# Expert weights in transfers of two experts, with eight experts' weights in memory

## What is computed

```python
logits = x @ gate_weight.T                      # 2048 tokens, 64 experts
scores = softmax(logits)
# the 3 best of 8 groups of experts are kept, and of these the 6 best experts of a token
flat = topk_i.reshape(-1)
pos = place of the token in its expert's queue
slot = flat * C + minimum(pos, C - 1)           # C = 96 places for each expert
buf = zeros((E * C, H)).at[slot].set(x[tok]).reshape(E, C, H)
g = einsum('ech,emh->ecm', buf, Wg)             # M = 176
u = einsum('ech,emh->ecm', buf, Wu)
out = einsum('ecm,ehm->ech', silu(g) * u, Wd)
y = sum over a token's 6 slots of out[slot] * topk_w
shared = (silu(x @ Sg.T) * (x @ Su.T)) @ Sd.T
return y + shared
```

## Time and profile before

| | us |
|---|---|
| median of 3 runs | 1223.92 |
| lowest and highest run | 1222.77, 1226.18 |
| the profiled execution, its time | 1213.88 |
| its span, from first to last instruction | 1212.1 |
| PE busy in the span | 1052.0 (87%) |
| mean granted clock of TensorE | 0.962 |

### The profile page before, as it was taken

One profiled execution on the slowest core, in us unless ns is written; L12 is line 12 of the kernel. 1 busy time (PEld: TensorE's weight loads), 2 busy tenths in 40 slices (PEclk: granted clock), 3 DMA queues, 4 the chain that ended last, 5 costly groups with the idle time before them and its releaser, 6 DMA issues.

```text
span 1212.1 us, 17812 instructions
## 1 busy us (share of the span) xinstructions
PE 1052.0 (87%) x5809; PEld 868.6 (72%) x5809; DVE 629.9 (52%) x1225; ACT 487.4 (40%) x864; POOL 401.6 (33%) x593
## 2 busy tenths in 40 slices
PE   4749999999999899999999999999787978777774
PEld 4538998898888789989788889888554545444443
DVE  3525455648586566678655767855564211111116
ACT  1315555555454445554544555544220122222220
POOL 2112222223225722222662322284106144344440
PEclk9969999999999999999999999999988998999995
DMA  9950000000001200000110000002010288999966
GB/s 367 328 179 0 0 0 0 1 1 27 11 1 45 90 1 1 35 1 1 66 48 1 1 36 1 1 18 89 9 44 3 63 218 212 225 226 227 232 141 211
DMA packets 58757, 95.74 MB, mean 79 GB/s; under 512 B 7771, under 2 KB 41318, under 8 KB 58176
## 3 DMA queue, kind: packets, MB, share of 16 engines
q1 hardware_dynamic: 46880, 80.66, 21.0%
q0 software_dynamic: 11808, 14.16, 6.2%
HBM read 62.17 MB, written 40.67 MB: 85 GB/s over the span
## 4 chain that ended last, share of the span: by engine, by line
PE 62%; DMA 12%; DVE 7%; issue 6%; POOL 6%; SPq 5%; ACT 2%; POOLq 0%; DVEq 0%; ACTq 0%
PE ps L1081 18%; PE ps L1104 9%; DMA wds<-in_wd 9%; PE ps L1128 9%; PE ps L1117 7%; PE ps L1286 4%; POOL slot_rows L436 3%; PE ps L1301 3%; PE ps L1223 2%; SPq L288 2%; PE ps L1233 2%; PE ps L1090 2%; PE ps L1111 2%; PE ps L1093 2%; DMA acc<-zrow 2%
## 5 line engine op out<-in xcount | busy, mean ns | idle before, releaser
L382 POOL TENSOR_TENSOR holdp<-neghalf 128x1 f32<-128x1 f32 x139 | 30.4, 219 | 554.6 <-DVE ss L728 270.7
L526 ACT ACTIVATE prob<-ps,rn 128x512 f32<-128x512 f32 (+3 forms) x256 | 121.1, 525 | 183.2 <-PE ps L1104 183.0
L1081 PE MATMUL ps<-wh,hth 128*128 128x384 f32 x512 | 178.0, 348 | 9.8 <-DVE wl L693 4.6
L728 DVE TENSOR_REDUCE ss<-arena 128x8 f32<-128x1024 f32 x64 | 78.1, 1220 | 199.9 <-ACT arena L510 199.6
L1128 PE MATMUL ps<-vx,prob 128*128 128x129 f32 (+1 forms) x1280 | 155.8, 277 | 22.1 <-POOL prob L430 21.9
L1128 PEld LDWEIGHTS ps<-vx,prob 128*128 128x128 f32 x1280 | 154.6, 193 | 25.9 <-POOL prob L430 23.2
L1081 PE MATMUL ps<-wl,hth 128*128 128x384 f32 x512 | 172.0, 336 | 0.0
L1081 PE MATMUL ps<-wh,htl 128*128 128x384 f32 x512 | 172.0, 336 | 0.0
L1104 PE MATMUL ps<-qt,kt 128*128 128x512 f32 (+3 forms) x512 | 152.8, 442 | 19.8 <-DVE arena L747 13.0
L510 ACT ACTIVATE arena<-ps 128x1024 f32<-128x1024 f32 x64 | 65.5, 1023 | 246.5 <-PE ps L1081 246.5
L489 POOL DMA_INDIRECT acc<-wos,arena x64 | 90.1, 1408 | 146.0 <-ACT wos L628 97.7
(11 more groups left out here) (161 smaller groups left out, 1608.3 us busy)
## 6 DMA issues: line engine op xcount, KB each, us to landing
wgus<-in_wgu SPq DMA_DIRECT2D x64, 352.0 KB
wds<-in_wd SPq DMA_DIRECT2D x64, 176.0 KB
slot_rows<-pay SPq DMA_DIRECT2D x1, 7728.0 KB, 35.4
arena<-slot_rows SPq DMA_DIRECT2D x64, 120.8 KB, 3.1
warena<-in_wqkv SPq DMA_DIRECT2D x1, 4992.0 KB, 20.1
acc<-zrow SPq DMA_DIRECT2D x2, 2048.0 KB, 29.5
warena<-acc SPq DMA_DIRECT2D x8, 512.0 KB, 7.4
wos<-in_wo SPq DMA_DIRECT2D x1, 2048.0 KB, 28.3
```

The costliest lines, as they stand in the source:

```text
L526: act_(prob[:, OFF[j]:OFF[j] + w], sflat[:, OFF[j]:OFF[j] + w], ACT.Tanh, scale=rn[:, bass.ds(head(n), 1), TT + j:TT + j + 1].squeeze(1)). ...
L728: nc.vector.tensor_reduce(ss[:].rearrange("p (c i) -> p i c", c=2), sq, X, ALU.add).then_inc(s["ss_rdy"], 1)
L1081: last = mm(ps[:, i, 0:3 * DH], hp[:, k, i * P:(i + 1) * P], wp[:, k, :], start=(k == 0 and m == 0), stop=(k == KC - 1 and m == 2))
```

## The change

The weights are packed in pairs: `wgu` holds two experts in one row of 1408 words for each of 128 partitions, and `wd` two experts in one row of 1024 words, padded from 88 rows to 96 (MP), the last 8 of zeros that no matmul reads. One transfer brings the weights of one kind for two experts, 704 KB and 384 KB. Four pairs are held (WR = 8 experts): two in the old arrays `wgus` and `wds`, which keep their sizes but for the rows of `wds`; the other two in memory of attention that is dead by then: the gate and up pairs in `prob` and in `arena2` behind the rows, the down pairs in `wos` (heads 4 to 7) and in `vx`. The first two pairs are loaded at the start as before; the other two where attention ends, behind two waits more in SP's queue (`o_rdy`: PE's last product with `prob`; `x2_rdy`: the last use of `yacc`). In the loop a pair is loaded at odd u alone, when its second expert is done, and it is for the next turn of eight.

```diff
+WR = 8
+MP = 96
...
-        wgus = sb("wgus", [P, RING, KC, 2 * M])
-        wds = sb("wds", [MC, RING, 2, D])
+        wgus = sb("wgus", [P, 2, 2 * KC * 2 * M])
+        wds = sb("wds", [MP, 2, 4 * D])
...
+        wg_pair = [wgus[:, 0], wgus[:, 1], prob[:, 0:4 * KC * M], arena2[:, XR * RW:XR * RW + 4 * KC * M]]
+        wd_pair = [wds[:, 0], wds[:, 1], wos[0:MP, 4:8, :].rearrange("p a d -> p (a d)"), vx[0:MP, 1024:1024 + 4 * D]]
+        wg_of = [wg_pair[u // 2].rearrange("p (a k m) -> p a k m", a=2, k=KC)[:, u % 2] for u in range(WR)]
+        wd_of = [wd_pair[u // 2].rearrange("p (a m d) -> p a m d", a=2, m=2)[:, u % 2] for u in range(WR)]
...
-        w_in = [sem(f"w_in{i}") for i in range(RING)]
+        w_in = [sem(f"w_in{i}") for i in range(WR // 2)]
...
-            for u in range(RING):
-                sp.dma_start(wgus[:, u], wgu[u]).then_inc(w_in[u], 16)
-                sp.dma_start(wds[:, u], wd[u]).then_inc(w_in[u], 16)
+            for u in range(2):
+                sp.dma_start(wg_pair[u], wgu[u]).then_inc(w_in[u], 16)
+                sp.dma_start(wd_pair[u], wd[u]).then_inc(w_in[u], 16)
...
+            sp.dma_start(wd_pair[2], wd[2]).then_inc(w_in[2], 16)
+            sp.wait_ge(s["o_rdy"], B * H)
+            sp.dma_start(wg_pair[2], wgu[2]).then_inc(w_in[2], 16)
+            sp.dma_start(wd_pair[3], wd[3]).then_inc(w_in[3], 16)
+            sp.wait_ge(s["x2_rdy"], 2 * B)
+            sp.dma_start(wg_pair[3], wgu[3]).then_inc(w_in[3], 16)
             sp.wait_ge(s["hmod"], 2 * B)
...
-            def gate_up(base, u):
-                sp.wait_ge(s["gu_ps"], base + (u + 1))
-                sp.dma_start(wgus[:, u % RING], wgu[bass.ds(base + (RING + u), 1)].squeeze(0)).then_inc(w_in[u % RING], 16)
+            def gate_up(r, u):
+                sp.wait_ge(s["gu_ps"], r * XR + (u + 1))
+                sp.dma_start(wg_pair[u // 2], wgu[bass.ds(r * 4 + (WR // 2 + u // 2), 1)].squeeze(0)).then_inc(w_in[u // 2], 16)
...
-            def down(base, u):
-                sp.wait_ge(s["dn_ps"], base + (u + 1))
-                sp.dma_start(wds[:, u % RING], wd[bass.ds(base + (RING + u), 1)].squeeze(0)).then_inc(w_in[u % RING], 16)
+            def down(r, u):
+                sp.wait_ge(s["dn_ps"], r * XR + (u + 1))
+                sp.dma_start(wd_pair[u // 2 % 4], wd[bass.ds(r * 4 + (WR // 2 + u // 2), 1)].squeeze(0)).then_inc(w_in[u // 2 % 4], 16)
...
-                if not (last and u >= XR - RING):
-                    gate_up(base, u)
+                if not last and u % 2 == 1:
+                    gate_up(r, u)
                 if not (first and u < 2):
-                    if not (last and u - 2 >= XR - RING):
-                        down(base, u - 2)
+                    if u % 2 == 1 and not (last and u >= 2):
+                        down(r, u - 2)
                     last_row(base, u - 2)
...
-                pe.wait_ge(w_in[e % RING], 32 * use)
+                pe.wait_ge(w_in[e % WR // 2], 32 * use)
                 for k in range(KC):
-                    last = mm(ps[0:C, 1 + e % 2, 0:2 * M], xgt[:, e % 2, k, :], wgus[:, e % RING, k, :], start=(k == 0), stop=(k == KC - 1))
+                    last = mm(ps[0:C, 1 + e % 2, 0:2 * M], xgt[:, e % 2, k, :], wg_of[e % WR][:, k, :], start=(k == 0), stop=(k == KC - 1))
...
-                    last = mm(ps[0:C, 4 + e % 2, 0:D], actt[:, e % 2, m, :], wds[:, e % RING, m, :], start=(m == 0), stop=(m == 1))
+                    last = mm(ps[0:C, 4 + e % 2, 0:D], actt[:, e % 2, m, :], wd_of[e % WR][0:MC, m, :], start=(m == 0), stop=(m == 1))
...
-                gu(e, base, (XR // RING) * r + (e // RING + 1))
+                gu(e, base, r + 1)
```

More of the change, by code:

```diff
@@ L336, in last_row, with sp_period @@
                 sp.dma_start(o95_d[bass.ds(base + u, 1)], orow[C - 1:C, u % RING, :]).then_inc(o95s[u % RING], 16)
-            def down(base, u):
-                sp.wait_ge(s["dn_ps"], base + (u + 1))
-                sp.dma_start(wds[:, u % RING], wd[bass.ds(base + (RING + u), 1)].squeeze(0)).then_inc(w_in[u % RING], 16)
-            def sp_period(base, u):
-                first = isinstance(base, int) and base == 0
-                last = isinstance(base, int) and base == E - XR
-                if not (last and u >= XR - RING):
-                    gate_up(base, u)
+            def down(r, u):
+                sp.wait_ge(s["dn_ps"], r * XR + (u + 1))
+                sp.dma_start(wd_pair[u // 2 % 4], wd[bass.ds(r * 4 + (WR // 2 + u // 2), 1)].squeeze(0)).then_inc(w_in[u // 2 % 4], 16)
+            def sp_period(r, u):
+                base = r * XR
+                first = isinstance(r, int) and r == 0
+                last = isinstance(r, int) and r == E // XR - 1
+                if not last and u % 2 == 1:
+                    gate_up(r, u)
                 if not (first and u < 2):
-                    if not (last and u - 2 >= XR - RING):
-                        down(base, u - 2)
+                    if u % 2 == 1 and not (last and u >= 2):
+                        down(r, u - 2)
                     last_row(base, u - 2)
@@ L357, in _ @@
                 for u in range(XR):
-                    sp_period(r * XR, u)
+                    sp_period(r, u)
             for u in range(XR):
-                sp_period(E - XR, u)
+                sp_period(E // XR - 1, u)
             last_row(E - XR, XR - 2)
@@ L1362 @@
         "wgu": np.concatenate([a("L0_ffn_Wg"), a("L0_ffn_Wu")], axis=1).transpose(0, 2, 1)
-               .reshape(E, KC, P, 2 * M).transpose(0, 2, 1, 3),
-        "wd": a("L0_ffn_Wd").transpose(0, 2, 1).reshape(E, 2, MC, D).transpose(0, 2, 1, 3),
+               .reshape(E // 2, 2, KC, P, 2 * M).transpose(0, 3, 1, 2, 4).reshape(E // 2, P, 4 * KC * M),
+        "wd": np.pad(a("L0_ffn_Wd").transpose(0, 2, 1).reshape(E // 2, 2, 2, MC, D).transpose(0, 3, 1, 2, 4)
+                     .reshape(E // 2, MC, 4 * D), ((0, 0), (0, MP - MC), (0, 0))),
     }
```

## The result

The changed kernel is slower. Its median over 5 runs is 1235.66 us (1233.59 to 1238.77), that of the kernel before, also over 5 runs, 1222.77 us (1216.40 to 1226.18): a ratio of 1.0111, with a 95% interval of 1.0074 to 1.0148. In a later group of runs, on another chip, it is 1226.22 against 1210.79, 1.0110 (1.0064 to 1.0156). 44 us less were forecast, and 12.9 more came.

A forecast was written before the change was run, and what follows sets the result against it. The prediction took a too short ring of down weights to bound the kernel. 43.5 us less in the loop and 0.5 at the start made 44.0, so 1223.92 - 44.0 = 1180 us, with a range of 1166 to 1207.

The forecast's parts named there:

- What bounds the kernel now: Loop over experts: a too short ring of down weights makes a step 3.39 us; PE's own bound is 2.47.
- The wait that goes: Loop: with weights asked for eight experts ahead, the wait for them, behind a landing of 4.6 us, goes wholly.
- Next in line, the scatter: Loop: the next scatter to the same copy waits for the landing, 4.8 to 5.4 us, 2.5 to 2.8 a step.
- the third rival: Loop: the scatter lands only after a pair's burst; at a landing of 7.5 us, step 3.85, 1248 us; chance 0.05.
- Next in line, the rows: Loop: rows queued behind a pair land in 4.7 us, making a step 2.70 to 2.76 us; 2.7 taken.
- The DMA engines' work: Loop: weights, rows, padding and scatters take the engines 2.4 to 2.6 us a step, about as long as PE.
- The second rival: Loop: the DMA engines are full already, so a step cannot be under 3.08 us; 1200 us; chance 0.24.
- The sum: Loop 43.5 us and start 0.5 us make 44.0 us less, 1180 us as the median.
- no change: Rival, loop: rows or scatters hold the step at 3.32 us or more; 1222 us; chance 0.05.
- The start: Until the last fill of weights lands and POOL follows at 76.67 us: -0.5 us, between +0.2 and -1.2.
- The loads at the end of attention: The last two pairs' loads and their two waits, in an idle gap of SP, cost nothing.
- The carrying over to the median: Whole kernel: the median is 10.04 us above the profiled execution, and the difference of 44.0 us is the same there.

The follow-up runs named there:

- experiment 4: The changed kernel without the reloads of weights in the loop, all experts computing with the first eight's weights; one run, 1154.29 us, loop 148.3 us.
- variant 2: The changed kernel with one transfer for each expert and kind, asked for in every period; 1193.69 us, ratio 0.9853 to the kernel before, loop 188.9 us.
- experiment 3: The kernel before with only the down weights padded to 96 rows, ring of four kept; 1204.34 against 1210.63 us, ratio 0.9952, loop 199.3 us.
- experiment 5: The changed kernel without the accumulating scatters of the loop, GpSimd only counting the semaphore up; one run, 1187.92 us, loop 184.3 us.

## Why the prediction was wrong

**What bounds the kernel now**: right. The ring of four places was in the chain, and PE's bound of 2.39 to 2.56 a step holds at its lower end (experiment 4: 2.39). The depth is worth something: variant 2 differs from experiment 3 in depth alone (and in where the added places lie), and its loop is 10 us shorter.

**The wait that goes**: right. No wait of gate and up for weights is left.

**Next in line, the scatter**: here the prediction failed. It said that one of two scatters meets a burst, that the worse lands in 4.8 to 5.4 us, and that two steps need one landing and 0.2 us; so it put this wait at 2.5 to 2.8 us a step, about the rows' 2.7. Three things were wrong with it. The landing that counts is 6.6 us in the median, since the scatter's packets do not begin until most of what q1 has queued is through (4.2 us behind the start, against 2.0 without weights). Both scatters of a turn meet the burst, since SP's rows load waits for a scatter's landing and the pair stands right behind it, so that landing, burst and next scatters are locked together. And from a landing to the next scatter it is 0.85 us, not 0.2. That makes (6.6 + 0.85) / 2 = 3.7 us a step, where the 52 steps that were forecast at 2.7 took 3.70. The prediction's own sign of being wrong, that POOL waits for the scatters' landings in every period, came true for the first scatter of nearly every turn.

This is the third rival, and it was given 0.05. What was held against it, that each scattered row waits for one larger packet of the weights, misread the page. The Trainium skill ("DMA: Bandwidth & Descriptors", section "Queues, rings and completion order") has an engine drain a whole packet from one queue before it turns to another, and puts a packet typically at some 9 to 17 descriptors; the prediction put a single row in the packet's place. An engine's share of a pair is 8 rows of gate and up and 6 of down weights, so that as an estimate, with a row taken for a descriptor, the page would let about the whole share go first. This case's trace agrees with that and not with turns of single rows: 2.75 us without a packet of the scatter. The median of 4.8 was no evidence either, because with the short ring the bursts were smaller and two steps were 6.8 us long, so a landing of 5 was never late.

**Next in line, the rows**: the mechanism and nearly the size were right. A landing of 4.7 us behind a pair and under 3 else was forecast; it is 5.3 to 5.6 behind a pair and 2.1 else. The 4.7 was worked out from 400 GB/s, a rate of rows of 12 to 20 KB at the start of the program, which the loop never had. What failed is that this chain was taken as the longest.

**PE's clock** was missing from the sum. PE pauses, the granted clock goes to the lower level, and the next period takes 4 us instead of 2.4. A granted clock of 0.92 over the changed kernel's 220 us is 35 us at the lower level, 2 x 0.08 x 220; in the kernel before it is 0.98 over 209 us, 8 us, and 1.00 in its second trace, with nearly as much idle time in smaller pieces. In the changed kernel this adds little by itself: the step is accounted for by the landing and 0.85 us, in which PE has no part. It counts where PE is on the path, as in experiment 5. No run shows its share alone.

**The DMA engines' work**: right in that it is not the bound, since the share fell to 0.79. The second rival (engines full) was wrong.

**The sum.** For the 60 steps from the fourth expert on, 160.0 us were forecast, 203.5 were before, and 215.2 are after: 192.5 for 52 steps and 22.8 for the last 8, where 140.4 and 19.6 were forecast. Two sums of the rivals are off. With the last 8 steps at 2.45, the others must take 3.54, not 3.32, for no change (3.32 gives 1212, not 1222), so that by the prediction's own 0.2 a landing of 6.9 and not 6.6 costs all of the gain; and the step of 3.85 gives 1240, not 1248. **The start**: -0.5 was forecast within +0.2 and -1.2; POOL starts at 76.95 where it was 76.67, +0.3, a little outside; what made it was not looked into. **The loads at the end of attention**: nothing, as said; the store behind them is issued at 877.28 where it was 877.12. **The carrying over to the median**: the difference was taken as the same there. That is sound only since the 12 us between router and experts belong to neither kernel; the profiled execution of the kernel before had been without them, and its median, 9 us higher, suggests that others had them.

## What to carry to other kernels

A load that is not urgent can still be expensive: asked for in one large piece, it stood here ahead of the small transfers that were. Before transfers are made larger, list the small ones on a closed chain that share the engines (here the scatter and the rows), add the whole burst to their landing, not one row of it, add the time from a landing to the next issue (here 0.85 us), and see whether the chain still closes in time. More than two copies `acc` might loosen that chain; this was not tried. Depth and size of a ring are two changes: here depth and the 96 rows together gained 1.5 to 1.8%, and the pairs took that and 1.1% more.

## What was not expected of the hardware

- Behind a burst of weights the scatter did not get its turn: 2.75 us without a packet beside 193 of the other queue. Beside rows alone, both queues moved packets at once (119 and 112 in 2 us). With transfers half as large, asked for in every period, its median landing was 5.5 us instead of 6.6.
- From a scatter's landing to the start of the next one that waits for it: 0.85 us, in 20 of 21 turns.
- Down weights in 96 rows instead of 88, with 9% more bytes: 0.9952 of the time, the loop 6 us shorter.
- The clock by the shape of idle time: PE busy 163.31 of 209 us at 0.98 in the kernel before, 170.07 of 220 at 0.92 in the changed one, 161.71 of 185 at 0.94 without scatters, where the idle time is least of the three but comes in a few long pieces.
- Some 12 us without a cause that the profile shows, between router and experts, in either kernel: in all six traces on two of the chips, in none of the eight on another.
